# A rounding on VectorE beside the attention: a constant word spread over the row as second tensor, in place of an immediate

## The reference: what is computed

```python
def quant_dequant_act_1x128(x):
    E, M, K = x.shape
    xb = x.reshape(E, M, K // BLK, BLK)
    amax = jnp.max(jnp.abs(xb), axis=-1, keepdims=True)
    safe = jnp.maximum(amax, ACT_EPS)
    q = (xb * (FP8_MAX / safe)).astype(jnp.float8_e4m3fn)
    return (q.astype(jnp.float32) * (safe / FP8_MAX)).reshape(E, M, K)

x = x + _L0_attn_ref(_layernorm(x, axis=-1), wq, wk, wv, wo)
x = x + _L0_xattn_ref(_layernorm(x, axis=-1), ctx_2048)   # both arguments rounded as above
x = x + _L0_ffn_ref(_layernorm(x, axis=-1), ...)
```

## Time and profile before

| | us |
|---|---|
| Median of 3 runs | 1537.47 (1534.38 to 1539.71) |
| The profiled execution | 1532.99 |
| Its span | 1530.9 |
| TensorE busy | 1438.5 (94%) |
| VectorE busy | 1165.2 (76%) |
| GpSimd busy | 1030.6 (67%) |
| ScalarE busy | 974.5 (64%) |

### The profile page before, as it was taken

The page is one execution under the profiler, slowest core; times in us unless marked ns, Lnnn a source line. Parts: engine busy times, 40 slices in busy tenths (PEclk is TensorE's granted clock), DMA queues, the critical chain, the costliest instruction groups (busy, mean ns, idle before and its releaser), DMA issues.

```text
span 1530.9 us, 26946 instructions
## 1 busy us (share of the span) xinstructions
PE 1438.5 (94%) x8617; PEld 1269.2 (83%) x8617; DVE 1165.2 (76%) x2810; ACT 974.5 (64%) x2510; POOL 1030.6 (67%) x1057
## 2 busy tenths in 40 slices
PE   5999999999999999798999999888898999999997
PEld 3788888888878888687888878777797888999996
DVE  7688888887898887888888888888665754677773
ACT  4687777777677788577878768766241412555562
POOL 3787888887887889689798988854404131366663
PEclk9999999999999999899999999999999999999998
DMA  6445544334232433324244342503111011587772
GB/s 206 137 112 174 150 115 138 111 86 121 81 90 56 125 101 90 83 76 128 53 128 124 81 121 66 162 24 118 70 36 49 22 42 39 171 267 236 250 245 81
DMA packets 108620, 174.74 MB, mean 114 GB/s; under 512 B 20936, under 2 KB 42696, under 8 KB 108480
## 3 DMA queue, kind: packets, MB, share of 16 engines
q1 hardware_dynamic: 104448, 160.51, 36.0%
q0 software_dynamic: 3840, 12.25, 2.1%
q10 hardware_dynamic: 192, 0.26, 0.1%
HBM read 94.05 MB, written 33.18 MB: 83 GB/s over the span
## 4 chain that ended last, share of the span: by engine, by line
PE 74%; DVE 10%; ACT 8%; issue 4%; DMA 2%; POOL 1%; SPq 1%; DVEq 0%; POOLq 0%; ACTq 0%
PE bank L514 16%; PE bank L516 16%; PE bank L515 16%; PE bank L566 7%; PE bank L532 4%; PE bank L533 4%; PE bank L581 4%; PE bank L582 4%; ACT P L912 3%; PE bank L506 2%; DVE Zb L1358 2%; DVE PTl L1297 1%; ACT Otmp L918 1%; DMA Oraw<-in_wo 1%; DVE P L1256 1%
## 5 line engine op out<-in xcount | busy, mean ns | idle before, releaser
L912 ACT ACTIVATE P<-P,mn 128x512 f32<-128x512 f32 (+3 forms) x512 | 283.9, 561 | 174.8 <-DVE mn L1256 174.3
L1695 POOL TENSOR_TENSOR P<-P,ri 128x128 f32<-128x128 f32 (+3 forms) x512 | 358.2, 732 | 39.5 <-DVE ri L1245 27.6
L1256 DVE CUSTOM_DVE_ANT_0 P<-bank,mask 128x512 f32<-128x512 f32 (+3 forms) x512 | 228.2, 481 | 90.6 <-PE bank L533 89.6
L1297 DVE TENSOR_TENSOR PTl<-bank,PTh 128x512 fp32r<-128x512 f32 (+1 forms) x384 | 210.0, 595 | 5.6 <-ACT PTh L924 1.4
L924 ACT ACTIVATE PTh<-bank 128x512 fp32r<-128x512 f32 (+1 forms) x384 | 176.4, 527 | 24.5 <-PE bank L566 20.6
L532 PE MATMUL bank<-KT,QT 128*128 128x256 f32 (+2 forms) x512 | 166.4, 334 | 20.0 <-DVE mn L1256 19.9
L566 PE MATMUL bank<-ident,P 128*128 128x128 f32 x1280 | 171.4, 278 | 0.2 <-POOL P L1695 0.2
L514 PE MATMUL bank<-XT,Wh 128*128 128x512 f32 x384 | 164.3, 428 | 6.7 <-DVE XT L1227 3.5
L581 PE MATMUL bank<-PTh,VS 128*128 128x256 f32 (+2 forms) x512 | 160.6, 325 | 8.1 <-issue 3.1
L533 PE MATMUL bank<-KT,QT 128*128 128x256 f32 (+2 forms) x512 | 162.4, 326 | 0.0
L582 PE MATMUL bank<-PTl,VS 128*128 128x256 f32 (+2 forms) x512 | 154.6, 324 | 0.0
(11 more groups left out here) (229 smaller groups left out, 4141.0 us busy)
## 6 DMA issues: line engine op xcount, KB each, us to landing
RW<-in_wf SPq DMA_DIRECT2D x153, 256.0 KB, 3.5
QT<-qh SPq DMA_DIRECT2D x256, 64.0 KB, 2.0
QT<-ql SPq DMA_DIRECT2D x252, 64.0 KB, 2.0
Oraw<-in_wo SPq DMA_DIRECT2D x16, 512.0 KB, 4.9
KT<-KT SPq DMA_DIRECT2D x32, 256.0 KB, 3.1
Wraw<-in_wqkv SPq DMA_DIRECT2D x9, 768.0 KB, 4.9
xnx<-in_ctx SPq DMA_DIRECT2D x24, 256.0 KB, 3.7
saved<-Wh SPq DMA_DIRECT2D x7, 768.0 KB, 3.5
```

The lines of the kernel that those rows point to most:

```text
L912: e.activation(pq, pq, ACT.Exp, bias=mn[:, z, qb:qb + 1], scale=-1.0, accum_out=rs[:, z, qb:qb + 1]).then_inc(a_exp, 1)
L1256: e.tensor_tensor_reduce(P[:, z, off[qb]:off[qb] + k], bank[n % 2][:, 0:k], mask[:, 512 - k:512], -0.125, BIG, ALU.add, ALU.min, mn[:, z, ...
L1297: e.tensor_tensor(pt_part(PTl, part), bank[2 + part][:, 0:128 * n].rearrange("p (m n) -> p m n", n=128), pt_part(PTh, part).bitcast(F32), ...
L1695: e.tensor_tensor(pq, pq, ri[:, z, qb:qb + 1].to_broadcast([128, n]), ALU.mult).then_inc(g_norm, 1)
```

## The change

A tile `bits` of 128 x 2 is added. GpSimd fills column 0 with the word 0x7F800000 and column 1 with 1.5 * 2^20, by two memsets right behind the first memset of its list. The two VectorE operations of each block then read their constant from this tile, spread over 512 columns, as a second tensor: the bitwise and becomes a tensor_tensor, and the max and multiply becomes a scalar_tensor_tensor that keeps 2^-6 as its immediate. `steps_of` gets a wait on the two memsets. The values computed are the same.

```diff
+        bits = sb("bits", [128, 2])
@@ steps_of(j), y = YB[j % 4], q = Zb[:, j % 2, :]
-                e.tensor_scalar(q.bitcast(U32), y.bitcast(U32), 0x7F800000, None, ALU.bitwise_and).then_inc(v_bm, 1)
+                need.wait_ge(g_bits, 2)
+                e.tensor_tensor(q.bitcast(U32), y.bitcast(U32), bits[:, 0:1].bitcast(U32).to_broadcast([128, 512]),
+                                ALU.bitwise_and).then_inc(v_bm, 1)
@@ large_steps_of(j)
-                e.tensor_scalar(q, q, 2.0 ** -6, 1.5 * 2.0 ** 20, ALU.max, ALU.mult).then_inc(v_bq, 1)
+                e.scalar_tensor_tensor(q, q, 2.0 ** -6, bits[:, 1:2].to_broadcast([128, 512]), ALU.max,
+                                       ALU.mult).then_inc(v_bq, 1)
@@ gpsimd_engine
             e.memset(Zb[:, 0, :], 0.0).then_inc(g_zero, 1)
+            e.memset(bits[:, 0:1].bitcast(U32), 0x7F800000).then_inc(g_bits, 1)
+            e.memset(bits[:, 1:2], 1.5 * 2.0 ** 20).then_inc(g_bits, 1)
```

More of the change, by code:

```diff
@@ L267, in decoder @@
             sem(f"v_{n}") for n in ("own", "xn", "xt", "wq", "wo", "ri", "mask", "ra", "rb", "k1", "vl", "join", "pt", "x"))
-        v_bm, v_bq, g_badd, g_bq = sem("v_bm"), sem("v_bq"), sem("g_badd"), sem("g_bq")
+        v_bm, v_bq, g_badd, g_bq, g_bits = sem("v_bm"), sem("v_bq"), sem("g_badd"), sem("g_bq"), sem("g_bits")
         p_cmax, v_peak, d_peak = sem("p_cmax"), sem("v_peak"), [sem("d_peak_out"), sem("d_peak_in")]
```

## The result

Over 15 runs of each kernel the changed one took 1543.04 us in the median, the kernel before 1535.09: a ratio of 1.0062, 95% interval 1.0034 to 1.0091. The profiled execution took 1542.69 us (before 1532.99), span 1540.8.

The account below looks back on a forecast made before the run. TensorE was taken as the bound. 21.5 - 1.5 - 1.1 = 18.9 us off the profiled 1532.99 gave 1514.1; adding 2 for part of the gap to the median gave 1516 us, stated range 1509 to 1530.

Parts of the forecast that it names:

- What bounds the kernel now: Whole kernel: TensorE is the bound, the other engines have room, and each long VectorE wait for GpSimd is paid in full.
- the three waits: Three L1358 of 9.87, 5.5 and 5.5 us, waiting while GpSimd ran; removing them was to gain 21.5 us.
- Will the new form wait as long?: At the rounding's L1358: the two-tensor form waits at most for the running GpSimd operation, so the three become at most 1.3 us.
- Its witness, L1235: Two-tensor VectorE operation at the same place of the turn: nine of them, six met by L1701, at most 1.726 us.
- the first rival: At the rounding behind L1716: the long waits stay, nothing is gained and 1.5 us lost, 1539 us; chance 0.09.
- the L1363 of rows 8: An old-form rounding operation that began inside L1716 and got through at its end, so the long wait is no rule.
- A rule that speaks against it: VectorE against GpSimd in SBUF: by the skill's rule alone, the new form should wait as the old one did.
- What it adds on VectorE: At the 40 rounding operations: each grows from 0.39 to 0.68 us, 11.2 us in all, mostly hidden behind TensorE's other matmuls.
- 11 x 0.14 = 1.5 us: At the head of the turns: 11 operations near 1.7 us cost 0.14 each; those below 1.47 us cost nothing.
- What is given back: In turns behind the long waits: ScalarE no longer catches up during a wait, so 2 x 0.54 = 1.1 us come back.
- On GpSimd: GpSimd's operations that meet the new form: held at most 11.2 us longer over 60 turns, within its room, so taken as nothing.
- slower: the waits stay and the cover is gone: At the four L1695 and the transposes: these come late, all 11.2 us falls on TensorE's path, 1549 us; chance 0.07.

Follow-up runs that it names:

- 64 x 384 run: The kernel before with GpSimd's L1701 cut to 64 partitions and 384 columns, the rest of that addition left out; a single run, 1556.99 us beside 1539.46.

## Why the prediction was wrong

**What bounds the kernel now: right.** The price of the three waits, 21.5 us by the differences of turns, is borne out by the kernel with L1716 widened: there the three turns are shorter by 10.48, 5.35 and 5.51, 21.3 us in all. The whole gain is 22.8 us between the medians, and 23.1 between turns 62 and 127 of the profiled executions; most of the rest lies in the three turns behind the first wait. The prediction saw the stake and missed what moves it.

**"Will the new form wait as long?": the step that failed.** It concluded that the new form waits for the running operation at most, so that the three become 1.3 us. They took 9.78, 5.85 and 5.81, and a fourth took 4.04. Its witness, L1235, stood in another situation: it began inside L1701, on 128 partitions, never in a run with L1716. The text said so, under the first rival, "no two-tensor operation of the trace began inside an L1716", and still took the absence as evidence. In the 64 x 384 run the same L1235 took 4.17. The counter-case that it used, the L1363 of rows 8, is a real exception, but it goes with the order of readiness, not with the form: all four old forms that got through asked before L1733 was ready, and so did the four new ones that met L1716 and took 0.98 to 1.02 us. The test that it set, a row of the new form above 2.5 us, has four such rows. What decides instead, as the runs show, is GpSimd's side: a 64-partition operation whose successor is ready to follow.

**"A rule that speaks against it".** The rule of the Trainium skill, "SBUF — State Buffer", section "Who interferes with whom", that a 2-port operation and one with two SBUF inputs both contend with GpSimd, gave the right result: both forms wait alike. The runs agree, 9.87 and 9.78 us in the same turn. What it says of how long, the other's whole instruction, holds for the seven roundings of before that met L1701 (at most 1.47 us), not for the long ones in a run with L1716.

**"What it adds on VectorE": the size of the operations right, the cover mis-sized.** 0.66 us undisturbed is near the 0.68 forecast, and 0.55 us behind GpSimd is as forecast. The term "11 x 0.14 = 1.5 us" measured 7.2 us. The 0.14 compared a turn with a 1.72 us operation (7.79) with one of another unit without one (7.65), and took turns with 1.44 us to cost nothing. Turn 68, the next of the same kind behind that of 7.65, took 7.52 with a rounding of 1.44 and 7.83 with one of 1.71: all 0.27 of the growth is paid, and no slack was in it. Nor do roundings below 1.47 cost nothing: with the operations cut to one column, the turns that had held one of 1.3 us became 0.64 and 0.67 us shorter. Some operations also came to meet a GpSimd operation that they had missed, 0.8 and 0.7 us in turns 75 and 99. The test named for it, more idle time of TensorE before L532, would have found little: 19.9 us became 23.1, most of it the new wait, since the loss shows as busy time. VectorE's busy time rose by 18.7 us instead of falling by 7.

**"What is given back": wrong as well.** The term, 1.1 us, had no occasion in the changed kernel, since the waits stayed. With L1716 widened the waits are gone, and nothing came back: the two turns in question, 91 and 115, took 7.63 and 7.39 us, where the prediction expected 8.19 in place of 7.65. The turns outside the three became shorter by 1.75 us in all, not longer.

**On GpSimd: near its bound, and harmless at L1695.** GpSimd's busy time rose by 10.8 us, where the prediction put at most 11.2, and the transposes that wait for L1695 began hardly later (0.2 us in all between the two kernels with L1716 widened). The wait on the memsets was taken apart by no run.

**The rivals.** What came true is the outcome of "slower: the waits stay and the cover is gone", 1549 us, with 7.2 of its 11.2 us: from the 1535.09 of before in the same set of runs, 1535.1 + 7.2 = 1542.3, against 1543.04. That sum leaves out the new wait, 3.3 us in the traces, so its closeness is partly luck. The path is not the rival's: it had L1695 and the transposes late, and the delay lies at the scores and the output product. It had 0.07; the waits that stay had 0.16 in all. The trace had three long waits in one situation and no two-tensor operation in that situation. With the rule of the Trainium skill beside it, that the waits stay should have been the likeliest case.

**The forecast's gain exists**, in another edit: 1509.92 us with L1716 on full rows, 1513.46 with a wait behind it, both in the old form.

## What to carry to other kernels

A witness counts only if it stood where the disputed operation will stand: look at what runs on the other engine before and behind, and at its widths, and if the trace has no such row, the form of the operation settles nothing. Where a VectorE operation waits for a whole string of GpSimd operations, look for one in the string that covers fewer partitions than the others, and widen it or make its successor wait for it. Price a longer operation by the same turn of the same kernel with a shorter one, not by turns of another unit; at the head of a turn of the bounding engine, take it as paid in full. And when an operation is cut to price it, look in the trace whether something else, here a DMA, took over.

## What the runs showed of the hardware

Not expected: a VectorE operation that meets GpSimd can wait for everything that follows without a gap, up to 9.9 us over ten operations, if a 64-partition operation is ahead of them and the next one is ready to follow, and one- and two-tensor forms do so alike (9.87 and 9.78 us; L1235 from 1.72 to 4.17). An addition of 512 columns on GpSimd takes 1.29 us on 64 partitions and on 128, so the narrow one saves nothing. At 256 columns the width alone decides between 0.90 and 2.49 us for the rounding that meets it. Shorter waits beyond the running operation also occur without a 64-partition one (L1204, 2.30 us; L1502, 2.1 to 2.6), and why is open.
